# Attention on one core: nine of sixteen key tiles as split pairs, three of them in the first chunk

## What is computed

```python
q = x @ (wq_codes * scales) + bq;  k, v likewise          # 2048 x 16 heads x 128
scores = einsum('bqhd,bkhd->bhqk', q, k) / sqrt(128)
attn = softmax(scores, axis=-1)
out = einsum('bhqk,bkhd->bqhd', attn, v)
return out @ wo + bo
```

## Time and profile before

| | |
|---|---|
| median of three timed runs | 2709.5 us (2706.68 to 2711.03) |
| the profiled execution | 2723.33 us |
| its span, first to last instruction | 2721.5 us |
| mean granted clock of PE | 0.980 of full speed |
| PE busy | 2601.6 us, 96% |
| POOL busy | 2184.8 us, 80% |
| DVE busy | 2108.0 us, 77% |
| ACT busy | 1663.2 us, 61% |

### The profile page before, as it was taken

One profiled execution on the slowest core, in us unless ns is written; L12 is line 12 of the kernel. 1 busy time (PEld: TensorE's weight loads), 2 busy tenths in 40 slices (PEclk: granted clock), 3 DMA queues, 4 the chain that ended last, 5 costly groups with the idle time before them and its releaser, 6 DMA issues. The chain is left out here.

```text
span 2721.5 us, 32565 instructions
## 1 busy us (share of the span) xinstructions
PE 2601.6 (96%) x11093; PEld 1884.1 (69%) x11093; DVE 2108.0 (77%) x2952; ACT 1663.2 (61%) x1914; POOL 2184.8 (80%) x1109
## 2 busy tenths in 40 slices
PE   7986899899999999999999999999999999997998
PEld 2333677677777777777777777777777777765777
DVE  6767657578888888888888888888888888887265
ACT  2233323367767776776777677677767766775155
POOL 2443789379988998998899899889988998997466
PEclk9898899999999999999999999999999999998999
DMA  2001566100000000000000000000000000003622
GB/s 69 0 0 53 157 168 167 60 12 5 12 1 20 8 5 16 5 9 5 20 5 8 16 5 9 4 17 4 13 12 9 9 5 9 1 5 80 235 68 57
DMA packets 76404, 92.66 MB, mean 34 GB/s; under 512 B 9342, under 2 KB 64881, under 8 KB 75986
## 3 DMA queue, kind: packets, MB, share of 16 engines
q1 hardware_dynamic: 73266, 83.36, 10.8%
q0 software_dynamic: 2976, 7.22, 0.8%
HBM read 64.43 MB, written 27.04 MB: 34 GB/s over the span
## 5 line engine op out<-in xcount | busy, mean ns | idle before, releaser
L1917 DVE TENSOR_TENSOR at_top<-at_psum_s,at_top 128x512 f32<-128x512 f32 x960 | 662.6, 690 | 213.3 <-ACT at_prob L1824 192.0
L1824 ACT ACTIVATE at_prob<-at_psum_s 128x1024 f32<-128x1024 f32 x512 | 521.4, 1018 | 450.5 <-PE at_psum_s L876 449.5
L2045 POOL TENSOR_TENSOR at_p_lo<-at_prob,at_p_hi 128x1024 fp32r<-128x1024 f32 x256 | 615.7, 2405 | 2.0 <-ACT at_p_hi L1838 2.0
L1906 DVE TENSOR_TENSOR at_prob<-at_prob,at_psum_m 128x1024 f32<-128x1024 f32 x512 | 603.5, 1210 | 0.0
L1830 ACT ACTIVATE at_prob<-at_prob 128x1024 f32<-128x1024 f32 x512 | 537.8, 1050 | 10.3 <-DVE at_prob L1906 7.2
L2074 POOL TENSOR_TENSOR at_acc<-at_acc,at_prob 128x1024 f32<-128x1024 f32 x189 | 453.1, 2397 | 84.0 <-ACT at_prob L1830 73.1
L1739 PE MATMUL at_psum_o<-at_prob,at_v 128*128 128x512 f32 x1024 | 482.8, 594 | 2.3 <-DVE at_oT_lo L1938 1.4
L2078 POOL TENSOR_TENSOR at_acc<-at_acc,at_prob 128x1024 f32<-128x1024 f32 x189 | 454.3, 2404 | 0.0
L874 PE MATMUL at_psum_s<-at_q_hi,sw_gate_up_hi 128*128 128x512 f32 x1024 | 402.1, 393 | 4.4 <-DVE sw_gate_up_lo L1898 4.4
L875 PE MATMUL at_psum_s<-at_q_lo,sw_gate_up_hi 128*128 128x512 f32 x1024 | 400.7, 391 | 0.0
L876 PE MATMUL at_psum_s<-at_q_hi,sw_gate_up_lo 128*128 128x512 f32 x1024 | 400.3, 391 | 0.0
(11 more groups left out here) (350 smaller groups left out, 4639.9 us busy)
## 6 DMA issues: line engine op xcount, KB each, us to landing
ef_gate_up<-in_ef_gate_up SPq DMA_DIRECT2D x8, 1024.0 KB
at_wq_split<-lf_pieces SPq DMA_DIRECT2D x8, 512.0 KB, 2.9
at_wk_split<-lf_pieces SPq DMA_DIRECT2D x8, 512.0 KB, 3.7
at_wv_split<-lf_pieces SPq DMA_DIRECT2D x8, 512.0 KB, 3.0
at_wo_split<-lf_pieces SPq DMA_DIRECT2D x8, 512.0 KB, 4.2
ef_down<-in_ef_down SPq DMA_DIRECT2D x8, 512.0 KB
ef_rows_in<-ef_zeros SPq DMA_DIRECT2D x23, 128.5 KB, 7.8
ef_rows<-ef_rows_in SPq DMA_DIRECT2D x23, 128.5 KB
```

The costliest lines, as they stand in the source:

```text
L1824: nc.scalar.activation(pair(u, c, half), psum_s[:, 2 * half:2 * half + 2, :], ACT.Copy).then_inc(kept, 1)
L1906: nc.vector.tensor_tensor(part, part, psum_m[:].unsqueeze(1).to_broadcast([P, 2, BT]), ALU.subtract).then_inc(shifted, 1)
L1917: nc.vector.tensor_tensor(top[:, u % 2, :], psum_s[:, t, :], top[:, u % 2, :], ALU.max).then_inc(maxed, 1)
L2045: nc.gpsimd.tensor_tensor(p_lo[:, at, :], part, p_hi[:, at, :].bitcast(F32), ALU.subtract).then_inc(p_lo_ready, 1)
```

## The change

PAIRED becomes (3, 2, 2, 2): the third tile of the first chunk is also a split pair. SPLITS says in how many pieces the splits of a chunk are made: two in the first, one in the others. In chunk 0, ACT makes a second, 128x512 high part after the second exponential, and POOL a second, 128x512 low part; PE waits for the second piece just before its third pair. POOL's order in chunk 0 becomes: both pieces of split_lo, then the sum. The room for p_hi and p_lo grows from four tiles to five. To find it, acc is given up: the sums of unit u go to the half of top that held the maxima of unit u + 1, after these have been transposed; and ones lies in acc2 at the start. The first maximum of a unit is taken over two tiles at once, from PSUM and from the copy that ACT kept, in place of a copy and a maximum. One of the value tiles of each group becomes a high and a low part as well.

```diff
-    PAIRED = (2, 2, 2, 2)
+    PAIRED = (3, 2, 2, 2)
+    SPLITS = tuple((n + 1) // 2 for n in PAIRED)
...
+    def splits_to(u, c):
+        return u * sum(SPLITS) + sum(SPLITS[:c + 1])
...
-            ones = sb("at_ones", [P, P])
...
-            acc = sb("at_acc", [P, BT])
+            ones = acc2[:, 0, 0:P]
...
+            def acc(u):
+                return top[:, (u + 1) % 2, :]
...
-                        pe.wait_ge(p_lo_ready, u * CH + c + 1)
                         at = PAIR_AT[c % 2]
                         for t in range(PAIRED[c]):
+                            if t % 2 == 0:
+                                pe.wait_ge(p_lo_ready, splits_to(u, c) - SPLITS[c] + t // 2 + 1)
...
-                    def split_hi(u, c):
+                    def split_hi(u, c, half):
                         n = u * CH + c
-                        act.wait_ge(exp_done, 2 * n + 1)
+                        act.wait_ge(exp_done, 2 * n + half + 1)
...
-                                if half == 0:
-                                    split_hi(eu, ec)
+                                if half < SPLITS[ec]:
+                                    split_hi(eu, ec, half)
...
-                            if c == 0 and t == 0:
-                                nc.vector.tensor_copy(top[:, u % 2, :], psum_s[:, t, :]).then_inc(maxed, 1)
-                            else:
+                            if c == 0 and t == 1:
+                                nc.vector.tensor_tensor(top[:, u % 2, :], psum_s[:, t, :], prob[u % 2][:, 0, :],
+                                                        ALU.max).then_inc(maxed, 2)
+                            elif c > 0 or t > 0:
...
-                        nc.vector.tensor_tensor(acc[:], top[:, 0], top[:, 1], ALU.add).then_inc(sum_ready, 1)
+                        nc.vector.tensor_tensor(acc(u), top[:, 0], top[:, 1], ALU.add).then_inc(sum_ready, 1)
...
+                        for half in range(SPLITS[c]):
+                            pool.wait_ge(p_hi_ready, splits_to(u, c) - SPLITS[c] + half + 1)
+                            tiles = slice(2 * half, min(2 * half + 2, PAIRED[c]))
+                            at = slice(PAIR_AT[c % 2] + tiles.start, PAIR_AT[c % 2] + tiles.stop)
+                            nc.gpsimd.tensor_tensor(p_lo[:, at, :], prob[u % 2][:, c * KPC + tiles.start:c * KPC + tiles.stop, :],
+                                                    p_hi[:, at, :].bitcast(F32), ALU.subtract).then_inc(p_lo_ready, 1)
...
                         if c == 0:
+                            split_lo(u, c)
                             pool.wait_ge(exp_done, n + 2)
                             if u >= 1:
                                 pool.wait_ge(sum_ready, u)
                             nc.gpsimd.tensor_tensor(acc2[:], pair(u, c, 0), pair(u, c, 1), ALU.add).then_inc(summed, 2)
-                            split_lo(u, c)
...
-                            if u >= 1:
-                                pool.wait_ge(w_ready, jobs["sum", u - 1] + 1)
-                            nc.gpsimd.tensor_tensor(acc[:], acc2[:, 0], acc2[:, 1], ALU.add).then_inc(sum_ready, 1)
+                            pool.wait_ge(w_ready, jobs["turn", u + 1] + 1)
+                            nc.gpsimd.tensor_tensor(acc(u), acc2[:, 0], acc2[:, 1], ALU.add).then_inc(sum_ready, 1)
```

More of the change, by code:

```diff
@@ L1754, in sum_rows @@
                         for t in range(TPB):
-                            last = nc.tensor.transpose(bank(key)[:, bass.ts(t, P)], acc[:, bass.ts(t, P)], ident[:])
+                            last = nc.tensor.transpose(bank(key)[:, bass.ts(t, P)], acc(u)[:, bass.ts(t, P)], ident[:])
                         last.then_inc(w_ready, 1)
@@ L1769, in _ @@
                     pe.wait_ge(bo_steps, 1)
-                    nc.tensor.matmul(psum_o[:, 0:D], ones[:], v_bias[:], start=True, stop=True).then_inc(bo_steps, 1)
+                    nc.tensor.matmul(psum_o[:, 0:D], ones, v_bias[:], start=True, stop=True).then_inc(bo_steps, 1)
                     project(0, 0, 0)
@@ L1830, in exp @@
                         nc.scalar.activation(part, part, ACT.Exp, scale=SCALE).then_inc(exp_done, 1)
-                    def split_hi(u, c):
+                    def split_hi(u, c, half):
                         n = u * CH + c
-                        act.wait_ge(exp_done, 2 * n + 1)
+                        act.wait_ge(exp_done, 2 * n + half + 1)
                         if n >= 2:
                             act.wait_ge(pv_done, n - 1)
-                        at = PAIR_AT[c % 2]
-                        nc.scalar.activation(p_hi[:, at:at + PAIRED[c], :], prob[u % 2][:, c * KPC:c * KPC + PAIRED[c], :],
+                        tiles = slice(2 * half, min(2 * half + 2, PAIRED[c]))
+                        at = slice(PAIR_AT[c % 2] + tiles.start, PAIR_AT[c % 2] + tiles.stop)
+                        nc.scalar.activation(p_hi[:, at, :], prob[u % 2][:, c * KPC + tiles.start:c * KPC + tiles.stop, :],
                                              ACT.Copy).then_inc(p_hi_ready, 1)
@@ L1957, in take_v @@
                         paired, plain, psum = v_tiles(key)
+                        if paired:
+                            dve.wait_ge(v_hi_ready, g * len(paired_jobs) + paired_jobs.index(n) + 1)
                         if plain:
@@ L2039, in split_lo @@
                         n = u * CH + c
-                        pool.wait_ge(p_hi_ready, n + 1)
-                        part = prob[u % 2][:, c * KPC:c * KPC + PAIRED[c], :]
                         if n >= 2:
                             pool.wait_ge(pv_done, n - 1)
-                        at = slice(PAIR_AT[c % 2], PAIR_AT[c % 2] + PAIRED[c])
-                        nc.gpsimd.tensor_tensor(p_lo[:, at, :], part, p_hi[:, at, :].bitcast(F32), ALU.subtract).then_inc(p_lo_ready, 1)
+                        for half in range(SPLITS[c]):
+                            pool.wait_ge(p_hi_ready, splits_to(u, c) - SPLITS[c] + half + 1)
+                            tiles = slice(2 * half, min(2 * half + 2, PAIRED[c]))
+                            at = slice(PAIR_AT[c % 2] + tiles.start, PAIR_AT[c % 2] + tiles.stop)
+                            nc.gpsimd.tensor_tensor(p_lo[:, at, :], prob[u % 2][:, c * KPC + tiles.start:c * KPC + tiles.stop, :],
+                                                    p_hi[:, at, :].bitcast(F32), ALU.subtract).then_inc(p_lo_ready, 1)
                     def split_shared(piece):
@@ L2080, in add_up @@
                             pool.wait_ge(summed, n + 2)
-                            if u >= 1:
-                                pool.wait_ge(w_ready, jobs["sum", u - 1] + 1)
-                            nc.gpsimd.tensor_tensor(acc[:], acc2[:, 0], acc2[:, 1], ALU.add).then_inc(sum_ready, 1)
-                    nc.gpsimd.memset(ones[:], 1.0).then_inc(bo_steps, 1)
+                            pool.wait_ge(w_ready, jobs["turn", u + 1] + 1)
+                            nc.gpsimd.tensor_tensor(acc(u), acc2[:, 0], acc2[:, 1], ALU.add).then_inc(sum_ready, 1)
+                    nc.gpsimd.memset(ones, 1.0).then_inc(bo_steps, 1)
                     pool.wait_ge(ln.norm_ready, first_norm.tiles + NT)
```

2 lines of the change are left out of this document (removed).

## The result

The changed kernel took 2717.1 us (median of 16 runs, 2712.2 to 2721.1), the kernel before 2709.4 (16 runs): a ratio of 1.0029, 95% interval 1.0021 to 1.0037, or 7.7 us slower. The forecast was 2712.5 within 2703 to 2720, with 0.26 for slower. The time lies in the range, but 4.6 us above the forecast. By the bound of 0.2% that the prediction set itself it is not the likeliest outcome ("same", 0.60) but "slower", and of the 0.26 for that, 0.20 stood for a dearer short split, which is not what happened.

The account below looks back on a forecast made before the run. PE was taken to bound the kernel on average, with POOL nearly setting the time in light runs. Seven cycles at -0.7 us in all plus the tail's +3.7 gave +3.0 on 2709.5: 2712.5 us, range 2703 to 2720.

Parts of the forecast that it names:

- a dearer short split: POOL's 128x512 split costs 1.47 us instead of 1.23, 25 times: +6.0, 2718.5 us; chance 0.24, of which 0.2 slower.
- POOL's saturated unit: POOL's period per attention unit without idle time goes from 27.89 to 29.02 us, against a PE unit of 27.33.
- PE's wait: In chunk 1 of the last of three neighbouring light units, PE waits 1.5 us for p_lo, once per 8 units.
- The old wait of 0.24: PE's present wait for p_lo in chunk 0, 0.24 us once per three light units, was to go.
- The tail: From unit 59 on: POOL's last sum 3.0 us later, plus the third tile's 0.70 in the last unit: +3.7.
- PE's gain: Chunk 0's third tile as three single passes goes from 0.86 to 0.70 us: about 0.17 saved per unit, 64 times.
- the parts that cost nothing: DVE's saved copy, ACT's added 0.60 us copy and the moved sums: nothing; constants and extra value tile: under 1 us.
- Rival (d): Chunk 0's third tile gives PE less than 0.17, a pair's first pass being held: 2714; chance 0.64 together with the main forecast.
- Per eight units: Per 8-unit cycle of attention: PE's work falls 1.36, the old 0.24 wait goes, 1.5 comes: -0.1 us; seven give -0.7.
- The start-up as nil: First three units of attention, where POOL starts up: PE saves 0.5 and may wait as much, so nil.
- Faster, by slack that I had misread: Slack before chunk 1 is 1.5 us more than read, so only the tail is paid: -8.9, 2700.5 us; chance 0.12.

## Why the prediction was right or wrong

**POOL's saturated unit, 29.02:** 29.09 measured. The short split is 1297 ns long and 1.24 to 1.26 us from the next start, where 1.33 would have decided the sign; I had taken 1.23. The rival of a dearer split is out.

**The place and size of PE's wait, 1.5 us in chunk 1 of the third light unit:** 1.4 there, and another 0.13 in chunk 2 of the unit before it, which I had not listed. The old wait of 0.24 is gone. This was the core of the forecast and its mechanism held; the two kernels with three tiles where POOL is idle or full show that it is POOL's load at that place. That the size came out too is in part luck, since two errors cancel. Counted from the start of the run's first PE unit, POOL's split ended at 81.52 us and not at 81.23: the run began 0.15 later than I had worked out and took 0.14 longer to that point. PE without a wait would have come 0.25 later as well, since its three steps won 0.07 to 0.09 each and not 0.17.

**The tail, +3.7:** the time from unit 59's exponentials to the next layer's first product went from 149.6 to 154.0, +4.4. POOL's last sum moved by 3.6 where I had 3.0: the three units behind unit 59's sum cost 3.9 more than before and not 3.4 (one sum began 0.43 us behind the end of the one before it, where 0.15 is usual), and the new order won 0.3 at the start of unit 59 and not 0.43. The third tile's 0.7 stands behind it.

**PE's gain, 0.17 per unit:** this is the term that failed most, and with it the place of ACT's copy among the parts that cost nothing. Without pieces the steps are 0.15 to 0.2 shorter than with two tiles, so the tile was sized nearly right. In the changed kernel only the steps with keys or certain values to make keep that; five of eight keep 0.07. I had written that "the first copy behind it, of the outputs, has room before PE's next use". It had no room, because I looked at the output's copy and not at the queries' copy between, on which DVE's whole next step is queued: a 0.66 us delay of one copy became 0.66 us for the low part of the output, and PE's load came 0.1 us late. Rival (d) had a smaller gain, but for another reason and with half the loss per step.

**Per eight units,** I had -0.1: -1.36 gain, -0.24, +1.5. Measured is 243.83 against 243.17, +0.66: the chunk 0 steps give -1.06 with the old wait in them, the two waits +1.51, the value step +0.28, and the small differences of other steps come to -0.07. Of the 0.76 that I was off, 0.29 is POOL's later end; the light run's own steps count for nothing, since PE waits for POOL at its end anyway; 0.2 is the gain missing in the two other steps, and 0.28 the value step. So ACT's copy explains 0.48 of it and POOL the rest, which is also why making the piece later gave back so little. Seven times 0.76 is 5.3; with the tail's 0.7 more and the start's 0.4 less that is the 5.7 us between the forecast +3.0 and the stretch's +8.7.

**The start-up as nil:** the first three units became 0.4 us shorter, but by luck: with two tiles they gain 2.7, and the third tile takes 2.3 of that. I had worked out neither.

**Faster, by slack that I had misread:** did not happen; the reading of one light run held for all of them.

**The range** held, but its upper part stood there for a dearer short split, not for what filled it.

## What to carry to other kernels

When an engine is bound on average and another is nearly so in a part of the period, an exchange between them is decided in that part: write down the second engine's saturated period, its lead where the part begins, and the deadline it meets last. With the same 24 third tiles the kernel was 0.37% slower than before where they stood in the units in which the second engine was full, and 0.22% faster where it had idle time, though most of that gain is the order's (two tiles alone give 0.18%). Idle time on an engine is no cover by itself: for an instruction that is put in, look at the one directly behind it in the program, who waits for it, and what is queued behind that.

## What the hardware showed that I had not expected

A DVE instruction of 128x512 with both operands in SBUF took 0.68 us beside an idle POOL and 2.82 to 2.90 us when POOL had just begun a 128x1024 one with two operands; with one operand in PSUM it took 0.68 at any time.

In the changed kernel PE waited 2.66 us for p_lo before unit 62's chunk 3, and in the stretch behind, the granted clock was 0.56, most of it at the lower level of 1.2 GHz; passes started 0.43 us apart in place of 0.23.

Busy time by stretch of the changed kernel, columns as before.
```profile
2452.72:2456.60 3.88, 3.88 (x14) 3.18 (x15) 0.45 (x1) 2.51 (x4) 3.80 (x3) 0.56 0.00 0
```
The kernel before, in two stretches: the earlier one, and the one that answers to the row above.
```profile
2447.50:2450.50 3.00, 3.00 (x6) 1.39 (x6) 3.00 (x4) 1.12 (x2) 2.98 (x2) 0.51 0.00 0
2455.40:2459.20 3.80, 2.52 (x15) 2.01 (x15) 2.41 (x3) 3.77 (x5) 3.72 (x3) 1.00 0.21 86
```
So the clock fell in both kernels near attention's end, before as well, behind a wait of 1.95 us for the last maxima. What differs is the place: before, PE had a wait of 0.74 us for p_lo and 1.27 for the last sum still ahead, and these could hide what it lost; after, the low clock reached up to the last sums. PE came to them 0.34 us after they were ready instead of 0.15, so this cost 0.2 us here. Why the clock fell where it did these runs don't show.
